# Turning attention's sums and the experts' rows in the DMA crossbar instead of on TensorE

## The chip, the cores and the metric

One NeuronCore of a Trainium2 chip runs the kernel. The metric is the device time of one execution in microseconds (us), the median of several runs. The engines are TensorE (PE, matrix products and transposes), VectorE (DVE), ScalarE (ACT), GpSimd (POOL) and SyncE (SP, which issues most of the DMAs). Each works through its own program in order and waits on semaphores for the others. PSUM is the memory that PE writes to; a transpose on PE ends there and has to be copied to SBUF by another engine. A crossbar transpose is a DMA that moves rows of 16-bit elements from SBUF to SBUF and turns them on the way; it needs neither PE nor PSUM.

## The reference, cut to what matters

```python
h = tokenizer(x)                       # 64 images: a class token and 4 patch tokens of 256 numbers
h = concatenate([h, txt], axis=1)      # 82 tokens an image, 64 images
xn  = layernorm(layernorm(h))          # attention: 16 heads of 16, relative bias from w_rel
q, k, v = split(xn @ w_qkv + b_qkv)
attn = softmax(q @ k.T * scale + bias)            # 82 x 82, per image and head
h = h + (attn @ v) @ w_out + b_out
xn  = layernorm(h)                     # experts: 8 of rank 64, two for each of the tokens 0 to 2047
for e in experts:                      # indices and weights are inputs
    ye = gelu(xn @ w1A[e].T @ w1B[e]) @ w2A[e].T @ w2B[e]
h = h + sum over the two experts of weight * ye
```

Everything is float32. 64 x 82 = 5248 token rows are 41 tiles of 128 rows. In the program's own inputs the experts' part applies to the first 2048 rows, 16 tiles.

## The kernel before, in words

The **tokenizer** (until some 119 us) works on 18 patch tiles and prepares the first quarter of attention. It is a block of its own: attention begins when all its engines are through. Near its end DVE normalises tiles 0 to 2 (`token_rows`), takes the statistics of tiles 3 to 5 (`token_stats`), and POOL normalises those (`xh`).

**Attention** is a loop over 64 blocks b, one image each. PE's order is written out by hand. In block b it makes `scores(b)` (L1303, 32 products into all of `psS`), `weigh(b-2)` (L1322, probabilities times values into the one bank `psO`), four `turn`s of the probabilities of block b-1 (L1312, into three banks of `psQ` that rotate), `turn_back(b-2)` (L1330), and between them the work on whole tiles: `xT` (L1271), `val` (L1290), `project` (L1346), and one quarter of keys and queries `qk` (L1280). Last comes `turn_att(b-2)` (L1337), two transposes of the divided sums `att`.

DVE subtracts the row maxima (`shift`, L1744 and L1746), divides the sums (`normalise`, L1763 and L1765), takes statistics and copies keys and queries out of PSUM (L1732). scores(b+1) waits until shift(b) has read `psS`; turn_att(b-2) waits for normalise(b-2), which DVE does behind shift(b). ACT makes the exponentials (L1588) and copies from PSUM: `oT` (L1566), `probT` (L1596), `hT`, `vs`, `po`, and `attT` (L1575), the two turned halves of the divided sums in a ring of 512 columns, from which `project` reads. weigh(b) waits until copy_attT(b-1) has emptied `psO`.

POOL normalises tiles (`prepare`, L1129 to L1135), adds the output row's bias to H (`add_row`, L1142), then the projection (`add_project`, L1148). For the first 16 tiles it also normalises rows for the experts into `fx` (L1159), and SP sends them to `normed_rows` in HBM. SP moves values `vs` to `vv` (L1067), loads the experts' weights, and sends finished rows to `out` (L1074).

The **expert loop** takes 39 tiles of gathered rows in 20 pairs p. POOL gathers the rows of a tile by a list (L1175). PE turns a pair (`pair_in`, L1421), ACT copies it to `pair_xT` (L1608), and PE makes `low` (L1437), `hidden` (L1452), `down` (L1467) and `result` (L1479); ACT makes the two gelu halves (L1625). DVE copies the pair's weights to their places: `own_wa` (L1774) and `own_wb` (L1782), the second of which waits until result(p-1) has used its buffer. POOL scatters the results to `entry_rows`; at the end they are read back, weighed and added.

## Time and profile before

| | us |
|---|---|
| median of 3 runs | 639.86 (634.64 to 640.08) |
| the profiled execution: time | 638.33 |
| the profiled execution: span, first to last instruction | 636.5 |
| tokenizer, until the first scores | 119.3 |
| blocks 0 to 63 of attention, first scores to last | 119.3 to 492.1 |
| expert loop, hidden(1) to the last results | 512.1 to about 609 |
| reading back, weighing, adding, sending | the rest |

The page gives each engine's busy time and its share of the span. PE's matrix products are pipelined, so that its share says how little it waits and not how near it is to its peak. The granted clock is 1.00 where TensorE runs at the higher of its two levels.

### The profile page before, as it was taken

The numbers are of one execution on the slowest core, as the hardware profiler recorded it, in microseconds if no ns is written. First come the engines' busy times: TensorE is split into PE (matmuls) and PEld (weight loads), VectorE is DVE, ScalarE is ACT, GpSimd is POOL, SyncE is SP. The second block draws the span as 40 slices with busy tenths as digits, with TensorE's granted clock in tenths as the row PEclk, the third lists the DMA queues.
The fourth block names the chain that finished last, engine by engine and source line by source line (L and its number), as shares of the span: only waits on it lengthen the run. The fifth ranks groups of instructions, "written<-read, shape, count | busy, mean of one in ns | idle before, by whom it ended". The sixth has DMA issues, their size and how long they took to land.

```text
span 636.5 us, 21150 instructions
## 1 busy us (share of the span) xinstructions
PE 587.2 (92%) x8302; PEld 494.7 (78%) x8302; DVE 492.4 (77%) x1023; ACT 368.9 (58%) x851; POOL 318.2 (50%) x407
## 2 busy tenths in 40 slices
PE   6989988789999999999999999999998899999940
PEld 5778866568888778888898889888887688888830
DVE  2766868689899988999899888988887566666516
ACT  1232134247766666776777667776777756666623
POOL 1520620668978567787744434564223177633330
PEclk9999999889999999999999999999999999999985
DMA  9990004011111117114343232222222033311138
GB/s 304 383 335 1 2 9 159 15 47 30 30 46 36 52 42 210 56 50 121 97 132 103 74 92 65 74 69 68 66 73 81 29 109 101 94 52 50 49 121 321
DMA packets 35629, 61.21 MB, mean 96 GB/s; under 512 B 6156, under 2 KB 21900, under 8 KB 35020
## 3 DMA queue, kind: packets, MB, share of 16 engines
q1 hardware_dynamic: 30732, 49.60, 24.3%
q0 software_dynamic: 4800, 10.27, 5.4%
q8 instruction: 67, 1.10, 0.7%
q14 instruction: 30, 0.25, 0.1%
HBM read 36.18 MB, written 18.00 MB: 85 GB/s over the span
## 4 chain that ended last, share of the span: by engine, by line
PE 67%; DVE 6%; issue 4%; DMA 1%; POOL 1%; ACT 1%; SPq 0%; POOLq 0%; DVEq 0%
PE psQ L1312 11%; PE psQ L1280 10%; PE psS L1303 7%; PE psS L1452 6%; PE psO L1322 6%; PE psO L1467 5%; PE psQ L1290 5%; PE psQ L1346 5%; PE psO L1330 4%; DVE mx L1744 2%; PE psQ L1437 2%; PE psQ L1421 2%; PE psO L1337 2%; PE psQ L1479 1%; PE psQ L1271 1%
## 5 line engine op out<-in xcount | busy, mean ns | idle before, releaser
L1596 ACT ACTIVATE probT<-psQ 82x328 f32<-82x328 f32 x256 | 110.1, 437 | 20.1 <-PE psQ L1312 18.5
L1744 DVE TENSOR_REDUCE mx<-psS 82x8 f32<-82x656 f32 x128 | 106.1, 829 | 11.9 <-PE psS L1303 11.4
L1312 PE MATMUL psQ<-ident_all,prob 82*82 82x82 f32 x1024 | 113.4, 237 | 0.6 <-DVE qk_space L1732 0.6
L1312 PEld LDWEIGHTS psQ<-ident_all,prob 82*82 82x82 f32 x1024 | 89.9, 120 | 28.1 <-issue 6.5
L1746 DVE TENSOR_TENSOR prob<-psS,mx 82x656 f32<-82x656 f32 x128 | 107.1, 837 | 4.4
L1588 ACT ACTIVATE prob<-prob 82x656 f32<-82x656 f32 x128 | 94.9, 742 | 3.2 <-DVE prob L1746 2.5
L1148 POOL TENSOR_TENSOR big<-big,po 128x256 f32<-128x256 f32 x41 | 29.9, 730 | 106.5 <-ACT po L1583 106.1
L1280 PE MATMUL psQ<-hT,wqkv 128*128 128x328 f32 (+10 forms) x320 | 81.0, 387 | 0.0
L1782 DVE COPY qk_space<-ex_weights 64x640 f32 x78 | 40.9, 524 | 35.7 <-PE psQ L1479 33.9
L1566 ACT ACTIVATE oT<-psO 128x328 f32<-128x328 f32 x64 | 28.4, 443 | 64.7 <-PE psO L1322 64.7
L1218 POOL DMA_INDIRECT entry_rows<-yv,slot_entry x39 | 39.3, 1009 | 41.4 <-ACT yv L1634 33.4
L1303 PE MATMUL psS<-qk_space 32*82 32x82 f32 x2048 | 54.0, 243 | 2.9 <-PEq L77 2.9
L1280 PEld LDWEIGHTS psQ<-hT,wqkv 128*128 128x128 f32 x320 | 50.2, 191 | 7.8
L1303 PEld LDWEIGHTS psS<-qk_space 32*82 32x82 f32 x2048 | 44.1, 150 | 9.6 <-issue 4.1
L1322 PE MATMUL psO<-probT,vv 82*32 82x82 f32 x2048 | 49.8, 238 | 0.8 <-ACT attT L1575 0.7
L256 PE MATMUL tk_ps<-cwT,big 128*128 128x256 f32 x180 | 42.3, 395 | 6.2 <-DMA big<-in_patches 5.6
L1135 POOL TENSOR_SCALAR xh<-big,a_mv,a_rst 128x256 f32<-128x256 f32 x35 | 42.9, 1225 | 6.0 <-PE psQ L1271 2.3
L1625 ACT ACTIVATE hT<-psS 128x1024 f32<-128x1024 f32 (+1 forms) x40 | 38.1, 1000 | 12.3 <-PE psS L1452 12.3
L256 PEld LDWEIGHTS tk_ps<-cwT,big 128*128 128x128 f32 x180 | 35.6, 199 | 12.2 <-DMA cwT<-in_conv_rows 5.6
L1175 POOL DMA_INDIRECT big<-normed_rows,slot_token x39 | 39.8, 1020 | 9.8 <-issue 8.0
L1290 PE MATMUL psQ<-wqkv,hT 128*128 128x256 f32 x164 | 43.7, 389 | 0.0
L1322 PEld LDWEIGHTS psO<-probT,vv 82*32 82x32 f32 x2048 | 37.9, 110 | 6.6 <-ACT probT L1596 1.0
(277 smaller groups left out, 1134.1 us busy)
## 6 DMA issues: line engine op xcount, KB each, us to landing
fused_rows<-in_txt SPq DMA_DIRECT2D x1, 4928.0 KB, 18.1
vv<-vs SPq DMA_DIRECT2D x24, 164.0 KB
big<-in_patches SPq DMA_DIRECT2D x2, 1600.0 KB, 10.7
out<-big SPq DMA_DIRECT2D x25, 128.0 KB, 3.6
big<-entry_rows SPq DMA_DIRECT2D x6, 512.0 KB, 6.7
ex_weights<-in_wa SPq DMA_DIRECT2D x8, 320.0 KB, 3.8
ex_weights<-in_wb SPq DMA_DIRECT2D x8, 320.0 KB, 5.4
normed_rows<-fx SPq DMA_DIRECT2D x16, 128.0 KB
```

Source lines behind the costliest of these rows:

```text
L256: mm = te.matmul(PS8[n % 2][:, 0:C], patches[:, n, q, :], cwT[:, q, :], start=(q == 0), stop=(q == 4))
L1135: pool.tensor_scalar(xh[:, n % 3, :], H[:, n, :], mv[:, n % 4, 0:1], rst[:, n % 4:n % 4 + 1], ALU.subtract, ALU.mult).then_inc(S["xh_ready ...
L1280: mm = te.matmul(bank(("qk", 4 * q + j))[:, lo:lo + size], wqkv[:, c, 128 * j:128 * j + 128], hT[:, c, a:a + size], start=(c == 0), stop=( ...
L1290: mm = te.matmul(bank(("val", n))[:, 0:C], hT[:, c, a:a + 128], wv[:, c, :], start=(c == 0), stop=(c == 1))
L1303: mm = te.matmul(psS[0:T, g, s:s + T], qT[rows, par, a, t, cols], kT[rows, par, a, t, cols], start=True, stop=True)
L1312: mm = te.transpose(bank(("turn", 4 * b + g))[0:T, s * T:s * T + T], prob[:, b % 2, g, s, :], ident_all[0:T, 0:T])
L1322: mm = te.matmul(psO[32 * k:32 * k + 32, s * T:s * T + T], vv[:, b % 4, h, :], probT[:, b % 2, h % 8 // 2, 2 * (h // 8) + h % 2, :], start ...
L1588: act.activation(prob[:, b % 2, 2 * half:2 * half + 2, :, :], prob[:, b % 2, 2 * half:2 * half + 2, :, :], ACT.Exp).then_inc(S["prob_ready ...
L1596: act.activation(probT[:, b % 2, g, :, :].rearrange("p s t -> p (s t)"), bank(("turn", 4 * b + g))[0:T, 0:4 * T], ACT.Copy).then_inc(S["pr ...
L1744: v.tensor_reduce(mx[:, half, :, :], s4, X, ALU.max).then_inc(S["max_ready"], 1)
L1746: v.tensor_tensor(prob[:, b % 2, 2 * half:2 * half + 2, :, :], s4, mx[:, half, :, :].unsqueeze(3).to_broadcast([T, 2, 4, T]), ALU.subtract ...
L1782: ins = v.tensor_copy(wb[RANK * h:RANK * h + RANK, p % 2, 640 * part:640 * part + 640], WB[RANK * part:RANK * part + RANK, bass.ds(e, 1), ...
```

## The change

Both transposes are taken from PE and given to DMAs that SP issues. A float32 number is two half-words, and the crossbar turns 16-bit elements, so the halves are kept apart as planes.

- **Divided sums.** DVE writes `att` into one of two buffers. ACT's `split_att(b)` copies its half-words into planes (4 x 128 a row, 82 rows of 96), SP's `turn_att(b)` turns the 96 x 512 plane rows into `attT_planes` (128 x 4 x 96), and ACT's `weave_att(b)` puts the half-words together in `attT`. In ACT's block b stand weave_att(b-3) and split_att(b-2), in place of copy_attT(b-2). weigh(b) waits for the division of block b-1. Everything behind `attT` is a block later: `projected(b)` takes tiles with last_of == b-4.
- **Experts' rows.** ACT's `split(n)` writes the normalised rows as planes, `normed_rows` holds half-words, and after the gather SP turns each half of a pair (128 x 512 half-words, 39 of them). ACT's `copy_pair` weaves from those planes and not from PSUM. Pairs 0 and 1 are copied within attention. `pair_in` is gone.
- **Order.** The last two projections stand behind hidden(1). POOL's `add_row` moves from behind `prepare` to `projected(b+1)`. The statistics of tiles 3 to 5 move ahead of DVE's last reading in the tokenizer, and one window's product (`dots`) from there into block 0 of attention. Some semaphores are joined, and the counts in waits follow.

```diff
 def projected(b):
-        return [n for n in range(NTL) if last_of[n] == b - 3]
+        return [n for n in range(NTL) if last_of[n] == b - 4]
...
-                if n >= 16:
+                if 16 <= n < 21:
                     dots(1, n - 14)
...
                     for k in range(3):
                         token_rows(k)
-            for k in range(3, 6):
-                token_stats(k)
+                    for k in range(3, 6):
+                        token_stats(k)
...
+            def turn_pair(p):
+
+                if p < 2:
+                    for k in range(2):
+                        sp.wait_ge(S["fx_sent%d" % k], 16 * NX // 2)
+                elif p < 4:
+                    sp.wait_ge(S["pair_turned%d" % (p % 2)], turned_pairs(p - 2))
+                    for k in range(4):
+                        sp.wait_ge(S["v_in%d" % k], 16 * v_pieces[NB - 4 + k])
+                else:
+                    sp.wait_ge(S["f_xT_ready"], p - 1)
+                for h in halves(p):
+                    j = 2 * p + h
+                    sp.wait_ge(S["xin%d" % (j % 8)], 16 * (j // 8 + 1))
+                    sp.dma_start_transpose(xT_planes(p)[:, h, :, :], row_words(R["xin_tiles"][j % RING])).then_inc(S["pair_turned%d" % (p % 2)], 16)
+
+            def turn_att(b):
+
+                if b >= 2:
+                    sp.wait_ge(S["attT_ready"], b - 1)
+                sp.wait_ge(S["att_split"], b + 1)
+                sp.dma_start_transpose(attT_planes[:, b % 2, :, :], att_planes[:, b % 2, :, :].rearrange("p k n -> p (k n)")).then_inc(S["att_turned%d" % (b % 2)], 16)
+
+            for b in range(-1, NB + 5):
+                if 3 <= b < NB + 2:
+                    turn_att(b - 3)
...
             for n in early[6:]:
                 prepare(n)
-            for n in early:
-                add_row(n)
...
                 for n in turned(b + 1):
                     if n not in early:
                         prepare(n)
-                        add_row(n)
+                for n in projected(b + 1):
+                    add_row(n)
...
-                te.wait_ge(S["attT_ready"], b)
+                te.wait_ge(S["att_ready"], 2 * b)
...
-            def turn_att(b):
-
-                te.wait_ge(S["att_ready"], b + 1)
-                for c in range(2):
-                    mm = te.transpose(psO[:, c * T:c * T + T], att[:, 8 * c:8 * c + 8, :].rearrange("p h d -> p (h d)"), ident_all[0:T, 0:T])
-                mm.then_inc(S["attT_ps"], 1)
...
             for p in range(1, NPAIR):
                 hidden(p)
+                if p == 1:
+                    project(NTL - 2)
+                    project(NTL - 1)
                 result(p - 1)
                 if p + 1 < NPAIR:
                     low(p + 1)
                 down(p)
-                if p + 2 < NPAIR:
-                    pair_in(p + 2)
...
+            def split_att(b):
+
+                act.wait_ge(S["att_ready"], 2 * b + 2)
+                if b >= 2:
+                    act.wait_ge(S["att_turned%d" % (b % 2)], 16 * (b // 2))
...
+                act.activation(att_planes[0:T, b % 2, :, :].rearrange("p (c l) n -> p c l n", l=2),
+                               att[:, b % 2, :, :].rearrange("p h e -> p (h e)").bitcast(U16).rearrange("p (c n l) -> p c l n", c=2, l=2),
+                               ACT.Copy).then_inc(S["att_split"], 1)
+
+            def weave_att(b):
+
+                act.wait_ge(S["att_turned%d" % (b % 2)], 16 * (b // 2 + 1))
...
                 for a, lo, size in pieces(T * b, T, RA):
-                    ins = act.activation(attT[:, :, a:a + size], psO[:, 0:2 * T].rearrange("p (c t) -> p c t", c=2)[:, :, lo:lo + size], ACT.Copy)
+                    ins = act.activation(attT_words[:, :, 2 * a:2 * (a + size)].rearrange("p c (t l) -> p c t l", l=2),
+                                         attT_planes[:, b % 2, :, lo:lo + size].rearrange("p (c l) t -> p c t l", l=2), ACT.Copy)
...
+            def split(n):
+
+                act.wait_ge(S["fx_normed"], n + 1)
...
+                act.activation(planes[:, n % 2, :, :].rearrange("p (k l) n -> p k l n", l=2), fx_words[:, n % 2, :, :, :].rearrange("p k n l -> p k l n"), ACT.Copy).then_inc(S["fx_ready"], 1)
...
+                if b >= 3:
+                    weave_att(b - 3)
                 if b >= 2:
-                    copy_attT(b - 2)
+                    split_att(b - 2)
+                for n in projected(b - 5):
+                    if n < NX:
+                        split(n)
+                if b in (NB - 4, NB - 2):
+                    copy_pair((b - NB + 4) // 2)
...
             def copy_pair(p):
                 n = len(halves(p))
-                act.wait_ge(S["f_xT_ps"], p + 1)
+                act.wait_ge(S["pair_turned%d" % (p % 2)], turned_pairs(p))
...
                 if b == 0:
-                    for k in range(NW - 1, NW):
+                    for k in range(NW - 2, NW):
```

How the instructions stand on PE at the end of an attention block (`prob` and `psQ` are turn, `att` the divided sums, `psS` the next scores). Before:

```order
L1280 MATMUL psQ<-hT,wqkv 128x328 x2
L1312 MATMUL psQ<-ident_all,prob 82x82 x4
L1337 MATMUL psO<-ident_all,att 128x82 x2
L1303 MATMUL psS<-qk_space 82x82 x16
L1322 MATMUL psO<-probT,vv 32x82 x16
```

Now:

```order
L1329 MATMUL psQ<-hT,wqkv 128x328 x2
L1361 MATMUL psQ<-ident_all,prob 82x82 x4
L1352 MATMUL psS<-qk_space 82x82 x16
L1371 MATMUL psO<-probT,vv 32x82 x16
```

The two transposes of `att` are gone, and scores follow turn directly.

On ACT at the same place, where `attT` was copied between the last `probT` of a block and `oT` of the next. Before:

```order
L1588 ACTIVATE prob<-prob 82x656
L1596 ACTIVATE probT<-psQ 82x328
L1575 ACTIVATE attT<-psO 128x2x82
L1566 ACTIVATE oT<-psO 128x328
L1596 ACTIVATE probT<-psQ 82x328
```

Now, in a block that also has a tile for the experts:

```order
L1616 ACTIVATE prob<-prob 82x656
L1624 ACTIVATE probT<-psQ 82x328
L1602 ACTIVATE attT<-attT_planes 128x2x164
L1591 ACTIVATE att_planes<-att 82x512
L1632 ACTIVATE yv<-fx 128x512
L1582 ACTIVATE oT<-psO 128x328
L1624 ACTIVATE probT<-psQ 82x328
```

One instruction has become two, in 16 blocks three. On PE, a step of the expert loop. Before:

```order
L1421 MATMUL psQ<-ident_all,big 128x128 x4
L1452 MATMUL psS<-fx,qk_space 128x128 x16
L1479 MATMUL psQ<-qk_space,fx 128x256 x2
L1437 MATMUL psQ<-pc,qk_space 64x128 x4
L1467 MATMUL psO<-hT,qk_space 64x128 x16
```

Now:

```order
L1474 MATMUL psS<-fx,qk_space 128x128 x16
L1502 MATMUL psQ<-qk_space,fx 128x256 x2
L1459 MATMUL psQ<-pc,qk_space 64x128 x4
L1489 MATMUL psO<-hT,qk_space 64x128 x16
```

The four transposes of a pair are gone, and hidden follows down.

## Rows read from the trace of the kernel before

**Rows 1.** The page, part 1: busy us, share of the span, instructions.

```profile
PE 587.2 (92%) x8302; PEld 494.7 (78%) x8302; DVE 492.4 (77%) x1023; ACT 368.9 (58%) x851; POOL 318.2 (50%) x407
```

**Rows 2.** The page, part 4: the chain that ended last, by engine.

```profile
PE 67%; DVE 6%; issue 4%; DMA 1%; POOL 1%; ACT 1%; SPq 0%; POOLq 0%; DVEq 0%
```

**Rows 3.** Windows: stretch, length, busy us, clock, DMA share, GB/s.

```profile
141.00:299.40 158.40, 157.29 (x2571) 131.98 (x2569) 144.91 (x288) 108.70 (x269) 121.68 (x159) 1.00 0.23 68
299.40:471.20 171.80, 171.70 (x2936) 147.75 (x2934) 153.83 (x277) 121.76 (x299) 81.85 (x110) 1.00 0.29 83
...
512.00:602.00 90.00, 90.00 (x1356) 78.90 (x1356) 55.01 (x118) 55.71 (x85) 49.41 (x50) 1.00 0.25 75
```

The busy times stand in the order PE, PEld (weight loads), DVE, ACT, POOL.

**Rows 4.** Groups by line: busy us, mean ns of one, idle before.

```profile
L1337 PE MATMUL psO<-ident_all,att 82*128 82x82 f32 x128 | 20.2, 239 | 2.8 <-DVE att L1765 2.7
...
L1337 PEld LDWEIGHTS psO<-ident_all,att 82*128 82x128 f32 x128 | 13.4, 141 | 4.5 <-DVE att L1765 4.4
```

**Rows 5.** Timeline at the end of block 30: start us, length us, engine.

```profile
309.96 0.45 PE L1312 MATMUL psQ<-ident_all,prob 82*82 82x82 f32 x4
...
310.51 0.20 PEld L1337 LDWEIGHTS psO<-ident_all,att 82*128 82x128 f32 x2 [0.28 <-DVE att L1765]
...
310.80 0.83 PE L1303 MATMUL psS<-qk_space 32*82 32x82 f32 x32
```

**Rows 6.** Groups by line: ACT's instructions by size.

```profile
L1588 ACT ACTIVATE prob<-prob 82x656 f32<-82x656 f32 x128 | 94.9, 742 | 3.2 <-DVE prob L1746 2.5
...
L1625 ACT ACTIVATE hT<-psS 128x1024 f32<-128x1024 f32 (+1 forms) x40 | 38.1, 1000 | 12.3 <-PE psS L1452 12.3
...
L1634 ACT ACTIVATE yv<-psQ 128x512 f32<-128x512 f32 (+1 forms) x20 | 11.6, 581 | 2.3 <-PE psQ L1479 2.3
```

**Rows 7.** Timeline: ACT between blocks 29 and 30.

```profile
305.12 0.29 ACT L1575 ACTIVATE attT<-psO 128x164 f32<-128x164 f32 x1
...
306.54 0.44 ACT L1566 ACTIVATE oT<-psO 128x328 f32<-128x328 f32 x1 [1.12 <-PE psO L1322]
```

**Rows 8.** One line each: SP's copies `vv<-vs`; landing of `out<-big`.

```profile
L1067 SPq DMA_DIRECT2D vv<-vs x104: 552/692/864, 123.0 to 485.9; - x104
...
DMA to landing us min/median/max: 2.1/3.6/7.6
```

The first gives the least, median and most ns that SP takes to issue one.

**Rows 9.** Timeline: from the tokenizer's end into block 1.

```profile
109.69 1.06 DVE L707 TENSOR_SCALAR xh<-big,a_mv,a_rst 128x256 f32<-128x256 f32 x3 [0.19 <-POOL a_rst L210]
...
112.03 0.43 DVE L700 BATCH_NORM_STATS2 a_stats<-big 128x6 f32<-128x256 f32 x1
...
115.19 3.63 POOL L216 TENSOR_SCALAR xh<-big,a_mv,a_rst 128x256 f32<-128x256 f32 x3
...
124.34 4.84 POOL L1142 TENSOR_TENSOR big<-big,out_row 128x256 f32<-128x256 f32 x7
...
131.55 0.20 PEld L1271 LDWEIGHTS psQ<-ident_all,xh 128*128 128x128 f32 x2 [2.62 <-POOL xh L1135]
```

**Rows 10.** Timeline at the end of block 61, without key and query work.

```profile
485.09 0.84 DVE L1746 TENSOR_TENSOR prob<-psS,mx 82x656 f32<-82x656 f32 x1
...
486.60 0.20 PEld L1337 LDWEIGHTS psO<-ident_all,att 82*128 82x128 f32 x2 [0.76 <-DVE att L1765]
...
486.90 0.83 PE L1303 MATMUL psS<-qk_space 32*82 32x82 f32 x32
```

**Rows 11.** Timeline: one step of the expert loop.

```profile
538.71 2.06 PE L1452 MATMUL psS<-fx,qk_space 64*128 64x128 f32 x32
538.82 0.60 ACT L1608 ACTIVATE pc<-psQ 128x512 f32<-128x512 f32 x1 [1.56 <-PE psQ L1421]
...
541.36 2.17 DVE L1782 COPY qk_space<-ex_weights 64x640 f32 x4 [1.90 <-PE psQ L1479]
...
543.47 0.66 PE L1421 MATMUL psQ<-ident_all,big 128*128 128x128 f32 x4
...
544.05 1.16 PE L1452 MATMUL psS<-fx,qk_space 64*128 64x128 f32 x16
```

More of the change, by code:

```diff
@@ L953, in attention_and_experts @@
     uses = [("xT", n) for n in range(3)] + [("qk", j) for j in range(4)] + [("val", 0)] + [("xT", n) for n in range(3, 6)]
-    for b in range(NB + 3):
+    for b in range(NB + 4):
         earlier = [("turn", 4 * (b - 1) + g) for g in range(HG)] if 0 <= b - 1 < NB else []
-        uses += earlier[0:1] + ([("pair", 1)] if b == NB else []) + [("xT", n) for n in turned(b)]
+        uses += earlier[0:1] + [("xT", n) for n in turned(b)]
         uses += [("val", n) for n in valued(b)]
-        uses += earlier[1:2] + [("project", n) for n in projected(b)] + ([("low", 0)] if b == NB else []) + earlier[2:3]
+        uses += earlier[1:2] + ([("project", n) for n in projected(b)] if b < NB else []) + ([("low", 0)] if b == NB else []) + earlier[2:3]
         uses += [("qk", 4)] if b == 0 else []
@@ L962, in attention_and_experts @@
         uses += [(kind, 0) for kind, at in LATE_USES if at == b]
-        uses += earlier[3:4] + ([("pair", 0)] if b == NB - 1 else [])
+        uses += earlier[3:4]
+    uses += [("project", NTL - 3), ("project", NTL - 2), ("low", 1), ("project", NTL - 1)]
     place = {use: k for k, use in enumerate(uses)}
@@ L1473, in result @@
                 te.wait_ge(S["t2_ready"], p + 1)
-                te.wait_ge(S["f_xT_ready"], min(p + 3, NPAIR))
+                if p == 0:
+                    te.wait_ge(S["psQ_act"], by_act["project", NTL - 1])
                 if p >= 1:
@@ L1526, in _ @@
             turn_back(NB - 1)
-            project(NTL - 2)
-            turn_att(NB - 1)
-            project(NTL - 1)
+            project(NTL - 3)
             down(0)
-            pair_in(2)
             for p in range(1, NPAIR):
                 hidden(p)
+                if p == 1:
+                    project(NTL - 2)
+                    project(NTL - 1)
                 result(p - 1)
@@ L1689, in _ @@
             copy_probT(NB - 1, 3)
-            copy_attT(NB - 2)
+            split_att(NB - 2)
+            weave_att(NB - 3)
             gelu(0, 0)
@@ L1694, in _ @@
             copy_t1(1)
-            copy_project(NTL - 2)
-            copy_attT(NB - 1)
-            copy_project(NTL - 1)
+            copy_project(NTL - 3)
+            weave_att(NB - 2)
+            split_att(NB - 1)
             copy_pair(2)
@@ L1700, in _ @@
                 gelu(p, 0)
+                if p == 1:
+                    weave_att(NB - 1)
                 gelu(p, 1)
+                if p == 1:
+                    copy_project(NTL - 2)
+                    copy_project(NTL - 1)
                 if p + 1 < NPAIR:
```

125 lines of the change are left out of this document (62 added, 63 removed).

## The prediction

> **What bounds the kernel now.** I read the busy times first [rows 1]: TensorE (PE) is busy 92% of the span, VectorE (DVE) 77%, ScalarE (ACT) 58%. Then the chain of waits [rows 2]: 67% of it is PE. So a shorter PE program is worth something, if nothing else takes over. Where something would is in the windows by stage [rows 3]. The first holds 26 attention blocks (3 to 28), the second 30 (29 to 58), the third 17 steps of the expert loop. A block lasts 158.4/26 = 6.09 us, then 171.8/30 = 5.73 us, with PE at 99% and 100% and its clock at 1.00. DVE works 144.91/26 = 5.57 us of the first and 153.83/30 = 5.13 us of the second, ACT 4.18 and 4.06 us. So DVE stands 0.5 to 0.6 us behind PE, ACT 1.7 to 1.9 us. In the expert stage DVE and ACT are busy 55 of 90 us, but I shall find there a cycle through DVE.
>
> The profiled execution took 638.33 us (span 636.5), 1.5 below the median of 639.86. I make the sum against 638.3 and add 1.5.
>
> **PE in a steady block.** The change removes the two transposes of the divided sums (`turn_att`): 128 instructions of 239 ns whose weight loads take 141 ns [rows 4]. What they take from the path is read at a block's boundary [rows 5]: after the four transposes of `turn` the weights of L1337 are loaded at 310.51, 0.28 us of it waited for DVE's `att`, and the next block's scores begin at 310.80. The two cost 0.29 us, and the wait goes too where there is one. I take 0.30 a block: 7.8 us in the first window, 9.0 in the second.
>
> Late next is DVE. It gains nothing, its chain of maximum, subtraction, division and statistics is untouched, and scores(b+1) still waits for shift(b). Blocks are uneven: those with few projections are short on PE and full on DVE. Against a DVE block plus some 0.15 us of hand-over, about a third of the cut finds no room: I keep 5.5 and 6.5 us.
>
> **ACT in a steady block.** It loses the copy of `attT` from PSUM, 0.29 us, and gets `split_att` (82 partitions x 512 half-words) and `weave_att` (128 x 328), both from SBUF to SBUF, and 16 times `split` (128 x 512). No row has half-words, so the price is bounded from rows of 32-bit elements [rows 6]: 1024 take 1000 ns, 512 take 581, so 0.82 ns an element; from SBUF 656 take 742 ns. By elements 512 half-words cost 742 - 144 x 0.82 = 624 ns, 328 cost 473. The lower end is by bytes (half: about 0.41 and 0.34), the upper is twice the time by elements. I take elements, because ACT's rows follow their number. Then a block gets 0.62 + 1.16 x (0.47 - 0.28) = 0.85 us more (1.16 for copies cut at the ring's end, 74 for 64 blocks), the first stage another 16 x 0.62/26 = 0.38. ACT reaches 4.18 + 0.85 + 0.38 = 5.41 of about 5.9 us in the first window and 4.91 of 5.5 in the second. In the order they stand between `probT` 3 and `oT` of the next block, exactly where ACT now has its largest hole [rows 7]: 0.29 of `attT`, then 1.12 us until weigh has run. Together 1.41 us, against 0.47 + 0.62 = 1.09: they fit with 0.3 us left. Where `split` follows, 1.71 do not fit, and `oT` and `probT` come 0.3 us late, part of it hidden by the value projection on PE. I take off 1.5 us in the first window and 1.0 in the second. **Steady blocks: -9.5 us** (4.0 + 5.5).
>
> **SP and the DMA.** The 64 crossbar transposes go to SP's queue, each ahead of that block's `vv` copies, and stop it until `split_att` is done. Those `vv` pieces are used two blocks later, so I cost that at nothing; if cover lacked, weigh would wait. The transpose has from the end of `split_att(b)` to `weave_att(b)`, one block on: 5.5 - 0.47 - 0.62 = 4.4 us, and 0.3 more that ACT has spare. The nearest rows [rows 8]: an SP copy takes 0.55 to 0.86 us to issue (median 0.69), and 128 KB land 2.1 to 7.6 us after the issue began, median 3.6. These 96 KB should need about 3.6, between 2.1 and 8.3 (7.6 behind an issue of 0.7). I take 3.6, nearest in size: hidden, with 1 us to spare. The Trainium skill (Advanced Engine Details and Errata, section X-Bar Transpose (TRN2)) says that transposing DMAs are as fast as plain ones; no row here shows it, and by it the sum stays as it is.
>
> **The first blocks.** `token_stats` 3 to 5 now start where `token_rows` end, at 110.75 in place of 112.03 [rows 9]. They gate POOL's three `xh`, which end at 118.82 and with them the tokenizer: -1.3 us. Then POOL adds the row to seven tiles, 4.84 us [rows 9], ahead of the next `xh`, for which PE's load waits 2.62 us. Their move to `projected(b+1)` frees that: -2.5. On DVE one window's product moves from the tokenizer into block 0, where DVE waits for PE's first keys and queries: nothing, or its own length once more if that cover is short. **-3.8 us** (bounds 1.3 and 5).
>
> **The last blocks.** Without key and query work PE waits for `att` [rows 10]: 0.76 us at 486.60. DVE's second subtraction ends at 485.93, the next scores start at 486.90. Without `turn_att` they can start at about 486.15 once `turn` is through: 0.75 us, three times. **-2.3 us.** Between the loops hidden(0) comes some 0.6 us earlier, and down(0) no longer waits for the last projections, which would be 2 us. But both come back in p = 1: result(0) waits for project(NTL-1), which waits for the last divided sums to be split, turned by a DMA of 3.6 us and woven behind gelu(1,0). **0, between -2 and +3.**
>
> **The expert loop.** A step lasts 5.34 us, from 538.71 to 544.05 [rows 11]. `pair_in` takes 543.47 to 544.05 = 0.58 us of PE. Without it hidden(p+1) could start at 543.47, but it also waits for `own_wb(p+1)` on DVE, which starts behind result(p-1), at 541.36, and ends at 543.53. With a hand-over of 0.15 the cycle through DVE is 543.68 - 538.71 = 4.97 us, so 0.35 of the 0.58 is won, 17 or 18 times. **-6.1 us** (PE alone would give 10.4). ACT's `copy_pair` grows from 512 elements to 1024 half-words, 0.6 to 1.0 us, but no longer waits for PE, and its idle 1.56 us [rows 11] hides it. Two crossbar transposes a step have two steps of time: cost nothing unless one lasts over 2.4 us of the queue.
>
> **Sum**: 638.3 - 9.5 - 3.8 - 2.3 - 0 - 6.1 = 616.6; with 1.5 for the median, **618 us**.
>
> **Rivals.** (a) *The crossbar lands late.* The only rival in which ACT waits every block. It decides at 4.4 + 0.3 = 4.7 us from `split_att` to landing: at 5.6 us ACT, and PE behind it, lose 0.9 us in 61 blocks: 618 + 55 = 673 us. For it: the median row is only 1 us short of it, the longest far beyond, and a transpose is not a copy. Against: no HBM at either end, and DMA engines are busy 23% to 29% here [rows 3]. (b) *Half-words are slow on ACT.* `weave_att` reads alternately from two planes 192 bytes apart, and `split` reads every second half-word. At twice the time by elements a block gets 1.17 us more than I took (0.62 + 1.16 x 0.47): ACT has 5.41 + 1.17 + 0.38 (`split`) = 6.96 us of work in the first window and 6.08 in the second and becomes the bound: 26 x 0.87 + 30 x 0.35 = 33 us over the old periods, less the 12 of the other parts: 661 us. Nothing in the trace speaks on strided half-words; all ACT rows follow the element count. The Trainium skill has a rule that speaks against the change here (SBUF — State Buffer, section Door 1: The DMA port swizzle): each access that crosses into another 16-byte line pays a penalty, and every read of the weave does; it names no size, and no run here shows one. (c) *The cut is worth nothing in the blocks*, because DVE and ACT together, each at 90%, are late in turn: only start, end and expert loop remain, 640 - 12 = 628; and if ACT then overruns its hole by 0.2 us in each of the 60 blocks (+12), 640. (d) *PE alone decides*: 7.8 + 9.0 + 2.3 + 3.8 + 10.4 = 33, 606 us.
>
> **Chances.** Forecast, with (c) at 628: 0.50. (d) 0.08. (c) at 640: 0.12. (b) 0.14. (a) 0.16. Below or above 1% (6.4 us, about what can be told from no change here): faster 0.58 (the forecast and (d)), within 0.12 (the later case of (c)), slower 0.30 ((a) and (b)). The range goes from 609, (d) less some of its chance, to 661, which takes in (b) and half of (a)'s nearer cases: some 0.18 is left out. The forecast's own range is 610 to 629.
>
> **What would show it.** Right: scores(b) to scores(b+1) of 5.4 to 5.5 us in the second window, PE's share still over 97% there, no wait of ACT's `attT` for a DMA; the new ACT groups at about 0.62, 0.47 and 1.0 us; the first xT of block 1 without its 2.6 us; expert steps of 4.97 us with hidden waiting for `own_wb`. Wrong: `attT` waiting for the crossbar (a); new ACT groups over 1 us and `oT` no longer waiting for PE (b); steps of 5.3 us or more in the expert loop, with ACT's `copy_pair` waiting for a DMA.

## The result, and the profile after

The changed kernel takes 675.9 us (median of 4 runs, 671.29 to 677.7), the kernel before 637.25 (4 runs): 1.0585 times as long, 95% interval 1.0534 to 1.0637. The forecast was 618. The profiled execution took 676.02 us, its span is 674.2, 37.7 more than before, at a mean granted clock of 0.949 (before 0.977). Below, medians are over all runs of a kernel, ratios leave out those that the chip disturbed.

The first rows are parts 1 and 4 of the page; they answer to [rows 1, 2].

```profile
PE 589.4 (87%) x8096; PEld 489.4 (73%) x8096; DVE 495.6 (74%) x1024; ACT 430.6 (64%) x931; POOL 316.3 (47%) x407
...
PE 38%; issue 16%; DMA 10%; DVE 6%; POOL 6%; ACT 3%; SPq 2%; ACTq 0%; POOLq 0%; DVEq 0%
DMA attT_planes<-att_planes 8%; PE psQ L1329 6%; PE psQ L1361 6%; PE psS L1474 4%; PE psS L1352 4%; PE psO L1371 4%; PE psQ L1388 3%; PE psO L1489 3%; POOL big L1227 3%; PE psQ L1339 3%; PE psO L1379 3%; DVE mx L1790 2%; POOL big L1194 1%; DMA big<-entry_rows 1%; DMA entry_rows<-yv,slot_entry 1%
```

PE's share of the chain fell from 67% to 38%, and the crossbar transposes alone hold 8% of it. The same stages as in [rows 3] (blocks 3 to 28, blocks 29 to 58, the expert loop from its third step):

```profile
139.10:309.00 169.90, 157.62 (x2521) 129.57 (x2520) 145.57 (x289) 132.33 (x306) 120.88 (x160) 0.98 0.30 77
309.00:500.00 191.00, 175.39 (x2873) 146.33 (x2872) 152.96 (x277) 144.54 (x332) 82.85 (x112) 0.96 0.37 92
565.30:643.00 77.70, 75.42 (x1182) 66.74 (x1183) 51.80 (x108) 57.52 (x77) 46.15 (x46) 1.00 0.65 128
```

Attention was 99% and 100% PE and is now 93% and 92%, ACT's 132 and 145 us of work are 78% and 76% of the stretches. Read from the first scores of blocks and the first products of hidden, the 37.7 us are:

| us | before | after | |
|---|---|---|---|
| until the first scores | 119.3 | 121.5 | +2.1 |
| blocks 0 to 2 | 21.7 | 17.6 | -4.1 |
| blocks 3 to 28 | 158.4 | 169.9 | +11.5 |
| blocks 29 to 58 | 171.8 | 191.1 | +19.3 |
| blocks 59 to 62 | 20.9 | 24.2 | +3.3 |
| last scores to hidden(2) | 25.3 | 36.0 | +10.7 |
| hidden(2) to hidden(19) | 89.9 | 84.5 | -5.4 |
| the rest | 29.2 | 29.4 | +0.2 |

The forecast had -4.0 and -5.5 where the table has +11.5 and +19.3. Most blocks last 4.4 to 7.2 us. Five last 10.8 to 12.6 (21, 27, 33, 36, 41). SP's timeline of the one at 290.25 (start, length, line):

```profile
280.99 1.20 SPq L1099 DMA_TRANSPOSE attT_planes<-att_planes  x1
282.92 5.05 SPq L1117 DMA_DIRECT2D vv<-vs  x3
288.01 0.45 SPq L1075 DMA_DIRECT2D ex_weights<-in_wa  x1
288.50 0.43 SPq L1076 DMA_DIRECT2D ex_weights<-in_wb  x1
288.97 0.43 SPq L1128 DMA_DIRECT2D normed_rows<-yv  x1
289.50 8.79 SPq L1099 DMA_TRANSPOSE attT_planes<-att_planes  x2
```

ACT and PE in the same block, in brackets the idle time before and what ended it:

```profile
286.56 0.61 ACT L1591 ACTIVATE att_planes<-att 82x512 uint16<-82x512 uint16 x1
...
290.62 0.42 ACT L1624 ACTIVATE probT<-psQ 82x328 f32<-82x328 f32 x1
296.01 0.51 ACT L1602 ACTIVATE attT<-attT_planes 128x328 uint16<-128x328 uint16 x1 [4.97 <-DMA attT_planes<-att_planes]
296.43 0.61 ACT L1591 ACTIVATE att_planes<-att 82x512 uint16<-82x512 uint16 x1
296.95 0.61 ACT L1632 ACTIVATE yv<-fx 128x512 uint16<-128x512 uint16 x1
297.47 0.42 ACT L1582 ACTIVATE oT<-psO 128x328 f32<-128x328 f32 x1
...
297.94 0.86 PE L1379 MATMUL psO<-ident_all,oT 128*82 128x128 f32 x3 [4.28 <-ACT oT L1582]
```

The split is done at 287.2. The transpose is issued 2.3 us later: the third `vv` copy waits for weigh of the next image, and 640 KB of loads and a store of 128 KB go out ahead of it. It lands 6.5 us after its issue began (by its semaphore, as everywhere in this text; where an expectation below has 1.9 us or 3.7 to 7.4, it counts to the end of the last packet, which comes earlier), ACT's `weave` is the first in its queue to feel it, and oT and turn_back wait behind. The clock row of that block, by windows (PE, PEld, DVE, ACT, POOL, then clock):

```profile
294.00:297.90 3.90, 0.00 (x0) 0.00 (x0) 1.87 (x3) 1.89 (x5) 1.07 (x4) 1.00 0.01 1
297.90:301.30 3.40, 3.36 (x13) 2.80 (x14) 0.67 (x2) 1.94 (x5) 2.23 (x3) 0.50 0.28 53
301.30:302.70 1.40, 1.40 (x9) 0.87 (x8) 0.18 (x1) 1.08 (x2) 0.66 (x1) 1.00 0.29 63
```

PE had nothing to do for 3.9 us and comes back for 3.4 us at a clock of 0.50, the lower level: 1.7 us more. In attention the clock is at 0.50 for 23.8 us in all, before for 6.8; at that rate the difference costs some 8.5 us (an estimate). The waits view over the whole run (us, times, longest):

```profile
ACT attT L1602 <- DMA attT_planes<-att_planes: 37.0, 19, 5.0
PE psO L1379 <- ACT oT L1582: 19.5, 8, 4.3
...
SPq L1117 <- PE psO L1371: 50.3, 20, 4.5
```

### The profile page after: what moved, and what is told of

The parts are those of the page before. It is cut to its first block, busy times and chain, and to the rows that moved or that the text cites. A ratio compares the mean times of both kernels' runs of the same rounds, so it can differ in the third digit from the quotient of the medians.

```text
span 674.2 us, 21047 instructions
## 1 busy us (share of the span) xinstructions
PE 589.4 (87%) x8096; PEld 489.4 (73%) x8096; DVE 495.6 (74%) x1024; ACT 430.6 (64%) x931; POOL 316.3 (47%) x407
## 4 chain that ended last, share of the span: by engine, by line
PE 38%; issue 16%; DMA 10%; DVE 6%; POOL 6%; ACT 3%; SPq 2%; ACTq 0%; POOLq 0%; DVEq 0%
DMA attT_planes<-att_planes 8%; PE psQ L1329 6%; PE psQ L1361 6%; PE psS L1474 4%; PE psS L1352 4%; PE psO L1371 4%; PE psQ L1388 3%; PE psO L1489 3%; POOL big L1227 3%; PE psQ L1339 3%; PE psO L1379 3%; DVE mx L1790 2%; POOL big L1194 1%; DMA big<-entry_rows 1%; DMA entry_rows<-yv,slot_entry 1%
## 5 line engine op out<-in xcount | busy, mean ns | idle before, releaser
L1361 PE MATMUL psQ<-ident_all,prob 82*82 82x82 f32 x1024 | 116.9, 242 | 12.5 <-ACT probT L1624 10.7
L1624 ACT ACTIVATE probT<-psQ 82x328 f32<-82x328 f32 x256 | 109.8, 435 | 25.9 <-PE psQ L1361 23.8
L1361 PEld LDWEIGHTS psQ<-ident_all,prob 82*82 82x82 f32 x1024 | 92.4, 124 | 44.3 <-issue 24.9
L1329 PE MATMUL psQ<-hT,wqkv 128*128 128x328 f32 (+10 forms) x320 | 82.9, 393 | 0.0
L1200 POOL TENSOR_TENSOR big<-big,po 128x256 f32<-128x256 f32 x41 | 30.2, 735 | 107.1 <-ACT po L1611 106.6
L1829 DVE COPY qk_space<-ex_weights 64x640 f32 x78 | 44.1, 565 | 31.5 <-PE psQ L1502 29.8
L1379 PE MATMUL psO<-ident_all,oT 128*82 128x128 f32 x256 | 41.9, 289 | 19.6 <-ACT oT L1582 19.5
L1602 ACT ACTIVATE attT<-attT_planes 128x328 uint16<-128x328 uint16 (+10 forms) x74 | 33.5, 465 | 37.1 <-DMA attT_planes<-att_planes 37.0
L1474 PE MATMUL psS<-fx,qk_space 64*128 64x128 f32 x624 | 44.3, 292 | 5.6 <-issue 5.6
L1474 PEld LDWEIGHTS psS<-fx,qk_space 64*128 64x128 f32 x624 | 40.9, 201 | 9.5 <-issue 9.5
L1388 PE MATMUL psQ<-wout,attT 128*128 128x256 f32 x164 | 47.2, 416 | 0.0
```

Source lines behind the costliest of these rows:

```text
L1329: mm = te.matmul(bank(("qk", 4 * q + j))[:, lo:lo + size], wqkv[:, c, 128 * j:128 * j + 128], hT[:, c, a:a + size], start=(c == 0), stop=( ...
L1361: mm = te.transpose(bank(("turn", 4 * b + g))[0:T, s * T:s * T + T], prob[:, b % 2, g, s, :], ident_all[0:T, 0:T])
L1379: mm = te.transpose(psO[0:T, s * 128:s * 128 + 128], oT[:, s, :], ident_all[:])
L1388: mm = te.matmul(bank(("project", n))[:, 0:C], attT[:, c, a:a + 128], wout[:, c, :], start=(c == 0), stop=(c == 1))
L1474: mm = te.matmul(psH[:, f // 4, h, f % 4 * 128:f % 4 * 128 + 128], wb[rows, p % 2, f * 128:f * 128 + 128], t1T[rows, p % 2, :], start=True ...
L1624: act.activation(probT[:, b % 2, g, :, :].rearrange("p s t -> p (s t)"), bank(("turn", 4 * b + g))[0:T, 0:4 * T], ACT.Copy).then_inc(S["pr ...
```

## The experiments

Theories: (1) the transposes are late in SP's queue, behind the `vv` copies' wait and the loads, and the clock adds to each stall; (2) the crossbar lands late beside other transfers; (3) ACT's added copies delay oT and probT; (4) the experts' half of the change costs between the loops what it saves in them. More came up on the way. All times are medians, those of the kernel before on the same chips 637.7 to 638.2.

**SP's order.** vv later, then loads ahead of vv:

```diff
-                for n in valued(b):
+                for n in valued(b - 1):
```
```diff
                     turn_pair(3)
+                load(b)
                 for n in valued(b - 1):
...
-                load(b)
```

> The changed kernel, 675.9 us, with SP's three copies of values (vv) one block later, so that they wait for products that are already made and no longer hold the transpose of the divided sums back. Theory 1 (the transposes are late because they stand in SP's queue behind those waits and loads; every long stall then halves TensorE's clock): the blocks of 10 to 12.6 us (starts 250.8, 290.2, 331.8, 355.5, 387.9) last under 7 us, ACT's wait for attT_planes falls from 37 us to under 12, and the time to 640 to 650. Rival 2 (the crossbar itself lands late beside other transfers): the waits for attT_planes stay near 30 us, the time above 665. Rival 3 (ACT's added copies make oT and probT late): blocks stay as they are, above 665.

653.5 us, ratio to before 1.0228 (1.0184 to 1.0271): 22 us back by one number. The blocks of 12 us at 290, 332 and 388 last 6.3 now, and ACT's wait for the crossbar is 22.0 us in 10. But three blocks last over 10 us (20, 31 and 58), and 640 to 650 was missed.

> As the last kernel, and SP issues the loads of the experts' weights right behind the transpose and ahead of the vv copies, so that they have most of a block to drain before the next transpose. Theory 1: a further 2 to 8 us, since no transpose finds 640 KB of loads ahead of it; 636 to 645 us. Rival 2: the weights' transfers slow the transposes wherever they are issued: within 2 us of the last kernel. A risk that both see: the vv copies now run behind the loads, and weigh waits for v_in; then slower by as many us.

649.4 us, but its runs lie between 641.3 and 655.5, so that the 4 us are not established. ACT still waits 20.2 us for the crossbar, 12 times.

**Which half, and which load.** The sums back on TensorE, all else of the change kept; then beside it the split, the transpose and a weave with nobody waiting; and two idle ACT copies in the kernel before:

```diff
-                if 3 <= b < NB + 2:
-                    turn_att(b - 3)
...
-                te.wait_ge(S["att_ready"], 2 * b)
+                te.wait_ge(S["attT_ready"], b)
...
+                if b >= 2:
+                    turn_att(b - 2)
```
```diff
                 if b >= 2:
                     copy_attT(b - 2)
+                    idle_weave(b - 2)
+                    idle_split(b - 2)
```

> The changed kernel with the divided sums turned on TensorE again (two transposes a block and ACT's copy of attT from PSUM), while the experts' rows stay on the crossbar and everything else of the change stays. Theory 1: all of the loss is in the sums' path, so the long blocks vanish, attention lasts as before (about 373 us from first to last scores), the start keeps its few us and the expert steps their 0.3 us each less what the waits behind the gathers take: 628 to 636 us. Rival 4 (a good part of the loss is in the experts' half of the change: transposes and copies of the pairs between the loops): over 645 us.

639.2 us, ratio 1.0006 (0.9975 to 1.0037). All of the loss is in the sums' path, but the experts' half wins nothing either: 89.9 us of steps became 84.9, and last scores to hidden(2) went from 25.3 to 30.2. My 628 to 636 was missed.

> As the last kernel, and beside it, for nothing, all the work of the changed path in its places: ACT's split of the divided sums, SP's crossbar transpose with its wait for the split, and a weave of other words; only nobody waits for the transposes (but the second split behind). ACT carries 0.33 us a block more than in the changed kernel, since it also copies attT from PSUM. Theory 1: ACT's load costs little and the transposes nothing while nobody waits: 3 to 15 us over the last kernel, and no block over 8 us in the steady part. Rival 3 (ACT's load): 25 us or more over the last kernel. Rival 2 (the transfers disturb the values, loads and gathers): long blocks remain, with waits for v_in or h_in.

648.0 us, ratio 1.0123 (1.005 to 1.0196): 9 us, of which one block (22, 10.6 us) is 4. That the steady part would have no block over 8 us was missed. The crossbar's work with nobody waiting costs 9 us, with its waits 37, and rival 3 (25 or more) does not hold.

> The kernel before, with two copies of half-words more on ACT in each block, right behind its copy of attT: a split of 82 x 512 and a weave of 128 x 328, on tiles that nobody else uses. No crossbar, no wait. They cost 0.62 + 0.54 = 1.16 us a block where the prediction found a hole of 1.12 us behind attT's own 0.29. Rival 3 (ACT's added copies are a good part of the loss): 15 us or more over the kernel before. Theory 1 (the loss lies in the order of SP's queue): under 8 us over it, since the copies lie in the hole; ACT's waits for weigh shrink from about 1.1 us to nothing.

637.1 us, ratio 0.9983 (0.9948 to 1.0019). 1.16 us a block more on ACT cost nothing. The row of its waits view, then that of the kernel before:

```profile
ACT oT L1568 <- PE psO L1324: 3.8, 8, 1.7
```
```profile
ACT oT L1566 <- PE psO L1322: 64.7, 64, 2.0
```

ACT's idle time in front of oT was 64.7 us, and the copies fill it. Rival 3 is out.

**The rhythm of the projections, and a block of slack.** In the change a projection always comes 4 blocks behind its last image; here 4 or 5, then 5 or 6 with the weave one block later:

```diff
+        free_at = [last_of[n] + d for d in (4, 5) if not proj_at or last_of[n] + d > proj_at[-1]]
+        proj_at.append(([b for b in free_at if b not in with_values] or free_at)[0] if n < NTL - 3 else last_of[n] + 4)
```
```diff
-                if b >= 3:
-                    weave_att(b - 3)
+                if b >= 4:
+                    weave_att(b - 4)
```

> The kernel with vv later and the loads first (649.4 us), and each projection 4 or 5 blocks behind its last image instead of always 4, so that it goes to a block without a value tile where there is one. Theory 5 (the change's move of the projections by one block put 25 of them, not 16 as before, into blocks that already have a value and an xT tile; 10 blocks are left with no tile at all, where PE has 4.4 to 4.5 us of work but DVE 5.2): the empty blocks go, and with them the blocks of 4.4 us beside those of 6.27; about 10 x 0.7 x half = 3 to 5 us less. Rival 6 (blocks average out, since DVE's share is carried over the block boundary): within 1 us.

648.7 us, ratio 1.0132 (1.0078 to 1.0186): no gain over 649.4 as a whole. Where nothing stalls there is one. Blocks 39 to 56 (18 blocks) by windows: the kernel before; sums on PE; loads first; weave later with spread projections.

```profile
357.50:460.40 102.90, 102.90 (x1757) 88.33 (x1756) 91.36 (x163) 73.12 (x181) 45.48 (x60) 1.00 0.24 68
```
```profile
356.40:461.10 104.70, 103.68 (x1761) 88.44 (x1760) 90.91 (x163) 73.44 (x181) 47.90 (x63) 1.00 0.27 69
```
```profile
358.80:460.60 101.80, 100.90 (x1722) 85.40 (x1720) 90.53 (x163) 86.90 (x198) 48.09 (x63) 1.00 0.38 89
```
```profile
358.50:458.80 100.30, 100.30 (x1722) 85.35 (x1720) 90.76 (x163) 86.55 (x198) 48.95 (x64) 1.00 0.40 90
```

A block is 5.72, 5.82, 5.66 and 5.57 us, each from one trace. So taking the transposes off PE is worth 0.16 (5.82 to 5.66), moving the projections one block later costs 0.10 (5.72 to 5.82), and spreading them gives 0.08 back. The reason is in the schedule: three blocks behind, 16 of the projections share a block with a value tile and from block 2 on no block is without one of the two; four behind, 25 do, and 10 blocks have neither. Six of these (26, 29, 37, 40, 51, 54) last 4.4 to 4.5 us in the changed kernel, where DVE's work in a block is 5.0 on average (90.53 us in 18).

> As the last kernel, with the weave one block later (4 blocks behind), and the projections 5 or 6, so that a transpose has some 10 us to land instead of 4.7. Theory 2 as far as it is true (landing of 3.7 to 7.4 us beside loads and stores still costs 20.2 us of ACT's waits): those waits fall under 5 us, all blocks but those that wait for other loads are at most 6.5 us, and the time is 8 to 15 us below the last kernel, less 1 to 2 us for one more weave between the loops. Theory 1 alone (all was SP's order, and that is mended): within 2 us of it.

633.8 us, ratio to before 0.9894 (0.9836 to 0.9952), 15 us under the last. ACT waits for the crossbar once, 3.8 us. So theory 2 was half of the truth: with SP's queue in order (the loads-first kernel) 13 of the 64 transposes still landed later than the 4.7 us of room, up to 8.2.

**The experts' half alone**, with projections three behind and the last two ahead of down(0), as before:

```diff
-        return [n for n in range(NTL) if last_of[n] == b - 4]
+        return [n for n in range(NTL) if last_of[n] == b - 3]
...
             turn_att(NB - 1)
+            project(NTL - 1)
             down(0)
```

> The changed kernel's experts' half alone: the divided sums on TensorE as in the kernel with sums on PE (639.2 us), and also the projections 3 blocks behind and the last two ahead of down(0), as in the kernel before. The start, the experts' rows and the expert loop are those of the change. From the spans: attention loses the 1.6 us that it had over the kernel before and wins the first blocks' 3; between the loops result(0) no longer waits for the late projections, so of the 4.9 us lost there 3 to 4 come back; the loop keeps its 5.0. Theory 5: 629 to 633 us, 1% faster than the kernel before. Rival 4 (the crossbar costs between the loops what it saves in them): 636 or more.

629.2 us, ratio 0.984 (0.9792 to 0.9887): the lowest median of all, 1.6% under the kernel before. Last scores to hidden(2) is 26.9 us.

**DMA packets held.** The weave-later kernel still has blocks of 10.4 and 11.7 us in which nothing waits for the crossbar. SP, PE and the windows of the second, from the gated kernel below, which has them at the same places:

```profile
336.75 2.18 SPq L1105 DMA_TRANSPOSE attT_planes<-att_planes  x1
339.03 0.52 SPq L1132 DMA_DIRECT2D out<-big  x1
339.60 0.43 SPq L1136 DMA_DIRECT2D normed_rows<-yv  x1
```
```profile
340.42 0.67 PE L1360 MATMUL psS<-qk_space 32*82 32x82 f32 x20
344.18 0.85 PE L1360 MATMUL psS<-qk_space 32*82 32x82 f32 x12 [3.09 <-issue]
```
```profile
340.00:342.00 2.00, 1.09 (x25) 0.78 (x23) 1.10 (x3) 1.78 (x4) 0.00 (x0) 1.00 2.01 72
342.00:344.00 2.00, 0.00 (x0) 0.00 (x0) 0.00 (x0) 0.00 (x0) 0.00 (x0) 0.91 0.20 63
344.00:346.00 2.00, 1.82 (x44) 1.65 (x44) 0.89 (x2) 0.00 (x0) 0.00 (x0) 0.50 0.51 141
```

PE stops in the middle of 32 products with no semaphore between them, and the DMA share is 2.01 (packets overlap) at 72 GB/s: in the packets' records 17 packets of 1 KB, one more than there are DMA engines, take 2.9 to 3.7 us each and end together at 343.9. I call that a hold; the longest packets of holds take 1.7 to 4.6 us. There is none in the trace of the kernel before. Over the four traces from vv later to weave later, a transpose with a store, or a load of `fused_rows` (rows of h), right behind it had one in 18 of 59 cases, one with a vv copy behind it in 1 of 131 at most. With a load of the experts' weights behind it none of 27 had one, but in four of those 10 to 14 packets of 2.5 KB took up to 1.7 to 2.0 us. Theory 7 makes the pair of transpose and store or load the cause, rival 8 the amount of traffic.

A third possibility is in the same records, and no run here separates it. The engines are not all held: in this hold packets of 2 KB, the size of a row of the vv copies, start six to a quarter of a us and take 0.09 us each, so that about two are moved at a time, and they are through at 343.2, some 0.7 us before the hold ends. Of the 59 cases 45 still had such packets starting between 1.2 and 2.2 us after the start of the transpose's issue; 17 of the 18 holds are among these. The hold may need three things: values still being copied, a transpose behind them, and a store or load behind that.

Idle transposes beside the experts' half alone, ahead of the stores or ahead of vv:

```diff
+                        turn_idle()
                         sp.dma_start(tokens[128 * n:128 * n + 128, :], H[:, n, :])...
```
```diff
                     sp.wait_ge(S["psQ_act"], by_act["val", n])
+                    turn_idle()
```

> The experts' half alone (629.2 us, sums on TensorE), with 41 crossbar transposes of unused words in SP's queue, each directly ahead of a store to out or normed_rows; nobody waits for them but the second next. Theory 7: all 16 DMA engines are held for 2 to 4 us several times, PE stops in such stretches and runs at half clock behind them, and the time is 8 to 30 us longer. Rival 8: at most one such stretch, within 3 us of 629.

> The experts' half alone (629.2 us) with the same 41 idle transposes, each directly ahead of the first vv copy of a tile (SBUF to SBUF), and so away from the stores. Theory 7: no stretch in which all DMA engines are held, time within 3 us of 629. Rival 8: as the last kernel.

635.9 us (ratio 0.9953, 0.9912 to 0.9994) with the transposes ahead of the stores, 631.0 (0.9882, 0.982 to 0.9944) ahead of vv. The size of theory 7's effect was overstated, and the two intervals overlap, so that 635.9 against 631.0 is not established. The traces differ: seven holds of 1 KB packets against none, though the second has one at 130.3 in which ten packets of 2 KB take 2.7 to 3.5 us. Block 22 takes 11.1 us in the first and 5.7 in the second. The places differ in one thing more: ahead of the stores 21 of the 41 transposes still had packets of values moving, and all seven holds are among those 21; ahead of vv only 3 of 41 had. So the amount of traffic alone (rival 8), which is the same in both, does not explain the holds, and whether the store behind or the values ahead of the transpose matters is not shown. The first one's PE there:

```profile
257.13 0.27 PE L1364 MATMUL psQ<-ident_all,prob 82*82 82x82 f32 x1
259.62 0.63 PE L1364 MATMUL psQ<-ident_all,prob 82*82 82x82 f32 x3 [2.22 <-issue]
```

The changed kernel itself, first with a gate, then with a wait for the landing:

```diff
+                if 2 <= b < NB + 2:
+                    sp.wait_ge(S["weigh_done"], min(b - 1, NB))
                 load(b)
```

> As the kernel with the weave a block later (633.8 us), and SP, once it has issued a transpose, waits for weigh of the running block (some 1.5 us) before it issues loads or stores. Theory 7 (a store or load of HBM issued right behind a crossbar transpose, while that is in flight, holds all DMA engines and the instruction supply for 2 to 4.6 us, and TensorE comes out of it at half clock): the blocks of 10.4 and 11.7 us (22 and 37) last under 7, the store-followed transposes land like the vv-followed ones (median 1.9 us instead of 3.3 to 4.7), and the time falls by 6 to 12 us, to 622 to 628. Rival 8 (such stretches come with the amount of traffic, wherever it stands): as many of them as before, the time within 2 us or higher, since the loads now start later.

636.5 us, ratio 0.9981 (0.994 to 1.0022), holds at the same places. The gate tested nothing: in 60 of 61 blocks weigh was through before the transpose was issued in full.

```diff
-                load(b)
                 for n in valued(b - 1):
...
+                if 3 <= b < NB + 2:
+                    sp.wait_ge(S["att_turned%d" % ((b - 3) % 2)], 16 * ((b - 3) // 2 + 1))
+                load(b)
```

> As the kernel with the weave a block later (633.8 us), and in each block SP issues loads and stores only when that block's transpose has landed, behind the vv copies. Theory 7 (a load or store of HBM issued while a crossbar transpose is in flight holds all DMA engines and stops TensorE): none or one of the six stretches of 1.7 to 4.1 us in attention is left, blocks 22 and 37 (10.4 and 11.7 us) last 5.4 to 6.5, and the time falls by 8 to 13 us, to 621 to 626. Rival 8 (they come with the amount of traffic): as many as before, within 3 us of 634.

647.0 us, ratio 1.0174 (1.0125 to 1.0224). No hold of 1 KB packets is left in attention, as theory 7 has it; with the loads behind vv and behind the landing, no store or load stands right behind a transpose in attention any more. The time was missed. The loads now go out late, directly ahead of the next transpose, which lands up to 8.1 us after the start of its issue, and ACT waits 15.6 us for it. And block 22 lasts 12.6 us without any hold: a load of `fused_rows` (1.4 MB, issued at 247.9, landed at 254.5) stands ahead of the vv copy issued at 250.5, whose last packets are in at 258.36, and weigh begins then:

```profile
258.45 0.90 PE L1379 MATMUL psO<-probT,vv 82*32 82x82 f32 x32 [4.47 <-issue]
```

So a long block is no sign of a hold by itself. Away from one neighbour the transfers run into the other.

**Between the loops.** The last two images' sums on TensorE, in the gated kernel; then the same in the kernel that waits for the landing, with pairs 2 and 3 transposed behind the last sums:

```diff
-                if 3 <= b < NB + 2:
+                if 3 <= b < NB + 1:
                     turn_att(b - 3)
...
+            turn_att(NB - 2)
             hidden(0)
```
```diff
-                if b == NB - 1:
+                if b == NB + 1:
                     turn_pair(2)
                     turn_pair(3)
```

> As the last kernel, with the divided sums of the last two images turned on TensorE and copied from PSUM, so that the last projections stand ahead of down(0) as in the kernel before and wait for no DMA. From the last scores to hidden(2) the kernel with the later weave takes 34.7 us, the kernel before 25.3, the experts' half alone 23.7. Expected: 26 to 28 us there, two projections more than before among them, so 6 to 9 us less than the last kernel; 614 to 622 us. Rival (the stretch is long because the expert loop's first transposes and weights come late): within 2 us of the last kernel, with ACT's copy_pair or DVE's own_wb at its head.

637.5 us (630.4 to 643.4), ratio 0.9905 (0.9868 to 0.9942). 614 to 622 was missed: last scores to hidden(2) takes 33.5 us, 34.8 before the edit. (The 23.7 that I set for the experts' half was misread; it is 26.9.) ACT's last weave waited 5.28 us for a transpose that SP issued behind four of the experts' rows, 5.2 us of issuing.

> As the last kernel, with the last two images' sums on TensorE and the transposes of pairs 2 and 3 issued behind those of the last divided sums. Theory 1 for the stretch between the loops (what is late there is again a transpose behind others in SP's queue): from the last scores to hidden(2) 26 to 28 us instead of 34, ACT's weave waits less than 1 us for the crossbar, and the time is 5 to 8 us below the last kernel; 614 to 620 us, faster than both kernels. Otherwise: 33 to 34 us again.

637.0 us, ratio 0.9996 (0.9967 to 1.0025): missed. ACT's waits for the crossbar are down to 5.7 us in all, but the profiled execution takes 33.2 us in that stretch again, 13.7 of them at a clock of 0.50. It took 644.5 us, 7.5 over the median, so how long the stretch is otherwise, and why 614 to 620 was missed, stays open.

## Why the prediction was wrong

**The step that failed** is the one on SP and the DMA: "Those `vv` pieces are used two blocks later, so I cost that at nothing". I asked who waits for vv once it stands behind the transpose, not whom the transpose stands behind: vv's third piece waits for weigh of the next image and stops SP for up to 4.5 us (50.3 us in 20 waits), and with it the transposes behind it. One block later for vv alone gives 22 of the 38 us back. Another 15 come back when the landing gets a block more of room (648.7 to 633.8).

**The landing** (3.6 us taken, 4.7 the limit) has no one length. In the changed kernel the median of 64 is 2.8 us from the start of the issue, of which 1.2 is the issue. 28 land within 2.2 to 2.5 us. The Trainium skill (Advanced Engine Details and Errata, section X-Bar Transpose (TRN2)) has them as fast as plain DMAs; for these the trace agrees, against 2.1 at least and 3.6 at the median for stores of 128 KB [rows 8]. But 19 land after 3.5 us and 11 after 4.7, up to 9.0, beside loads, stores and copies of values. One median for a queue that carries 640 KB loads was the mistake. Rival (a) had the mechanism, but as a delay in every block; ACT waits in 19 of 64, longer, up to 5.0 us, and the clock adds to it, which I did not price: 3.9 us without work cost another 1.7.

**PE's cut** was priced at 0.30 a block, of which the forecast kept 0.17 (9.5 us in 56 blocks) because DVE and ACT would have no room for more. It is 0.16 where nothing stalls. That the kept number comes out is in good part luck, since PE itself wins no more than that. A boundary with the sums on PE, and one without (loads first):

```profile
379.20 0.45 PE L1350 MATMUL psQ<-ident_all,prob 82*82 82x82 f32 x4
379.49 0.30 PE L1375 MATMUL psO<-ident_all,att 82*128 82x82 f32 x2
379.72 0.83 PE L1341 MATMUL psS<-qk_space 32*82 32x82 f32 x32
```
```profile
386.71 0.45 PE L1361 MATMUL psQ<-ident_all,prob 82*82 82x82 f32 x4
387.09 0.83 PE L1352 MATMUL psS<-qk_space 32*82 32x82 f32 x32
```

From the start of turn to the start of scores it is 0.52 and 0.38 us, 0.14 less and not 0.30: part of turn_att stood where PE loses time anyway between the two.

**The projections' move** I took for neutral; it costs 0.10 a block, so that the net gain of a block without any stall is 0.06 us.

**ACT** was right: prices as taken, and idle copies cost nothing. By form (busy, mean ns):

```profile
L1591 ACT ACTIVATE att_planes<-att 82x512 uint16<-82x512 uint16 x64 | 39.5, 617 | 0.0
...
L1602 ACT ACTIVATE attT<-attT_planes 128x328 uint16<-128x328 uint16 x54 | 27.4, 508 | 30.1 <-DMA attT_planes<-att_planes 30.0
L1642 ACT ACTIVATE pc<-vs 128x1024 uint16<-128x1024 uint16 x17 | 20.0, 1175 | 0.0
```

624, 473 and 1000 ns were taken. Rival (b) is out; of the penalty for crossing 16-byte lines (the Trainium skill, SBUF — State Buffer, section Door 1: The DMA port swizzle) at most 7% and 17% can be in the last two.

**First blocks**: -4.1 in blocks 0 to 2, of which block 1 is 1.9 (6.97 to 5.10), against the -2.5 forecast there. Block 0's 1.5 are the clock: in the kernel before it is at 0.50 from 119.6 for 3.4 us, in this one from 113.5, ahead of the first scores. The tokenizer's -1.3 can't be seen: with the same tokenizer the first scores came between 117.8 and 124.4 us, as the clock fell or not.

**Between the loops** 0 was taken, -2 to +3; the experts' half as changed costs 4.9 there, the whole change 10.7. I named its chain (result(0) waits for the last projection, that for the last weave) but neither SP's four transposes of the experts' rows ahead of those of the last sums, 5.2 us, nor the clock, which is at 0.50 from 530.0 for 13.7 us.

**The expert loop** was -6.1 and is -5.4. Its end (hidden, `own_wb`, the next hidden with its weight load) and a step of its beginning, where ACT's `yv` waits for the scatter:

```profile
620.93 2.06 PE L1474 MATMUL psS<-fx,qk_space 64*128 64x128 f32 x32
623.57 2.05 DVE L1829 COPY qk_space<-ex_weights 64x640 f32 x4 [1.34 <-PE psQ L1502]
625.69 1.89 PEld L1474 LDWEIGHTS psS<-fx,qk_space 64*128 64x128 f32 x32 [0.18 <-issue]
625.72 2.06 PE L1474 MATMUL psS<-fx,qk_space 64*128 64x128 f32 x32
```
```profile
575.04 0.60 ACT L1669 ACTIVATE yv<-psQ 128x512 f32<-128x512 f32 x1 [1.19 <-DMA entry_rows<-yv,slot_entry]
```

Late steps take 4.79 us (4.97 taken). `own_wb` takes 2.05 us there where 2.17 was taken and ends at 625.62, 0.07 ahead of hidden's first weight load, so the cycle through DVE and PE's own work (5.34 - 0.58 = 4.76) come out alike, and which of the two bounds the step is not shown. Early steps take 5.15, a wait that the step on crossbar transposes "cost nothing" left out. DMA's share rose from 0.25 to 0.65.

## What to carry to other kernels

Work moved to a DMA has to be followed in its issuing queue both ways: who waits behind it, and what it now waits behind; a copy that may be late by two blocks can stop a transfer that may not be late at all. Give a transfer with a deadline the slack of the longest landing in the trace, not of the median, take that landing at the semaphore that its reader waits for, and count what PE's clock adds to each stall. And a part that "only" comes one block later can fall out of the rhythm that balanced the blocks: count how many tiles each block gets.

## What the hardware showed that I had not expected

SP needs 1.2 us to issue one crossbar transpose of 96 x 512 half-words, where a plain load takes 0.43 and the median vv copy took 0.69, so that four in a row close the queue for 5.2 us. With a store to HBM, or a load of `fused_rows`, issued right behind one, packets of 1 KB on about all 16 DMA engines can take 1.7 to 4.6 us. 17 of the 18 such holds in four traces, and all seven with idle transposes, came while packets of values were still moving two at a time, and none was left in attention once the transposes' landing was waited for. PE stopped for 2.1 to 3.1 us in the middle of its products in four holds. But it did so, for 2.0 to 2.3 us, three times without a hold of 1 KB packets too (261.0 in the kernel with idle split, transpose and weave; the last scores of the two kernels that wait for the landing); neither of the two traces without crossbar transposes has such a stop. What makes the holds, and whether they are what stops PE, is open, and so are holds of 256-byte packets, about 2 us, near the first pairs' transposes, whose cost is not known.
